# Reordering the opening transfers of a fused attention and feed-forward block, with three more fill products near its end

## The reference

```python
sa, ca, ga, sb, cb, gb = (silu(c) @ wmod) in six parts            # one row for each of 8 batches
h   = layernorm(x) * (1 + ca) + sa                                # x: (8, 512, 128), float32
q, k, v = split(h @ w_qkv.T)                                      # 16 heads of 8
p   = s(logits - max) / sum(s(...)),  logits = q @ k.T / sqrt(8)  # s: a cubic polynomial and its inverse
x   = x + gate(ga) * ((p @ v) @ w_out.T + b_out)
h   = layernorm(x) * (1 + cb) + sb
x   = x + gate(gb) * ffn(h)    # three layers of +1/-1 weights: 256 (h and -h) -> 512 -> 512 -> 128
```

## Time and profile before

| what | value |
|---|---|
| median of 3 runs | 701.52 us (701.29 to 701.98) |
| the profiled execution | 701.58 us |
| its span in the trace | 699.8 us |
| mean granted TensorE clock | 0.968 |
| VectorE busy | 641.1 us of the span |
| TensorE busy | 634.3 us |

### The profile page before, as it was taken

One profiled execution on the slowest core, in us unless ns is written; L12 is line 12 of the kernel. 1 busy time (PEld: TensorE's weight loads), 2 busy tenths in 40 slices (PEclk: granted clock), 3 DMA queues, 4 the chain that ended last, 5 costly groups with the idle time before them and its releaser, 6 DMA issues.

```text
span 699.8 us, 9639 instructions
## 1 busy us (share of the span) xinstructions
PE 634.3 (91%) x3059; PEld 253.8 (36%) x3059; DVE 641.1 (92%) x757; ACT 602.3 (86%) x622; POOL 599.0 (86%) x394
## 2 busy tenths in 40 slices
PE   6478989898889999899989999999989999997998
PEld 5123333233323343233523343233423343334366
DVE  6588999999999999999999999999999999998853
ACT  2367889998999989999999989999999989998832
POOL 8469888899989999899989999898989989797810
PEclk9575999999999999999999999999999999999999
DMA  6614112141115122332114112422214122101001
GB/s 175 193 48 166 47 53 62 61 167 46 42 40 175 49 55 78 121 107 58 51 42 168 52 54 75 151 77 58 69 43 159 43 57 72 53 10 28 16 13 31
DMA packets 37783, 53.62 MB, mean 77 GB/s; under 512 B 11308, under 2 KB 20804, under 8 KB 37732
## 3 DMA queue, kind: packets, MB, share of 16 engines
q1 hardware_dynamic: 36748, 51.81, 24.5%
q10 hardware_dynamic: 984, 1.19, 0.6%
HBM read 29.17 MB, written 18.36 MB: 68 GB/s over the span
## 4 chain that ended last, share of the span: by engine, by line
PE 55%; DVE 22%; issue 11%; ACT 8%; SPq 2%; DMA 2%; DVEq 0%; ACTq 0%
PE MB L523 13%; PE OP L601 12%; DVE mx L983 11%; PE Z L569 9%; DVE cub L974 9%; PE SA L584 8%; ACT sq L731 4%; PE MB L536 3%; PE MB L513 2%; ACT prob L745 2%; PE MB L494 1%; PE MB L611 1%; DMA parts_q<-SQ 1%; SPq L423 1%; ACT hid L786 1%
## 5 line engine op out<-in xcount | busy, mean ns | idle before, releaser
L1218 POOL TENSOR_TENSOR cub<-cub 128x2048 f32<-128x2048 f32 x127 | 456.9, 3604 | 40.1 <-DVE cub L974 39.8
L974 DVE SCALAR_TENSOR_TENSOR cub<-sq,Z 128x1024 f32<-128x1024 f32 x256 | 309.9, 1212 | 12.4 <-ACT sq L731 12.4
L731 ACT ACTIVATE sq<-Z,shift 128x1024 f32<-128x1024 f32 x256 | 282.3, 1117 | 43.7 <-PE Z L569 42.1
L983 DVE TENSOR_REDUCE mx<-SA 128x2 f32<-128x1024 f32 x248 | 302.1, 1218 | 12.6 <-PE SA L584 9.1
L745 ACT ACTIVATE prob<-cub 128x2048 f32<-128x2048 f32 x128 | 244.4, 1910 | 1.5 <-DVE cub L941 1.1
L584 PE MATMUL SA<-KH,QL 64*128 64x512 f32 x496 | 123.2, 493 | 28.8 <-DVE mx L983 25.0
L601 PE MATMUL OP<-prob,Vq 128*16 128x512 f32 x1024 | 135.1, 601 | 0.0
L569 PE MATMUL Z<-QH,KH 64*128 64x512 f32 x512 | 129.7, 503 | 5.7 <-DVE cub L974 5.5
L569 PEld LDWEIGHTS Z<-QH,KH 64*128 64x128 f32 x512 | 48.6, 186 | 183.1 <-DVE cub L974 126.8
L523 PE MATMUL MB<-hid,W 128*128 128x512 f32 x192 | 108.0, 645 | 0.0
L584 PEld LDWEIGHTS SA<-KH,QL 64*128 64x128 f32 x496 | 47.7, 188 | 109.2 <-DVE mx L983 83.6
(11 more groups left out here) (213 smaller groups left out, 526.0 us busy)
## 6 DMA issues: line engine op xcount, KB each, us to landing
QL<-parts_q SPq DMA_DIRECT2D x62, 128.0 KB, 2.6
KH<-parts_k SPq DMA_DIRECT2D x62, 128.0 KB, 2.7
QH<-parts_q SPq DMA_DIRECT2D x62, 128.0 KB, 2.7
parts_q<-SQ SPq DMA_DIRECT2D x28, 256.0 KB, 2.6
parts_k<-SK SPq DMA_DIRECT2D x28, 256.0 KB, 2.7
nd<-OT SPq DMA_DIRECT2D x124, 32.0 KB
QH<-mp SPq DMA_DIRECT2D x126, 4.0 KB
out<-y SPq DMA_DIRECT2D x7, 256.0 KB, 2.9
```

The costliest lines, as they stand in the source:

```text
L731: nc.scalar.activation(sq[:, h, :], Z[:, h, :], ACT.Square, bias=shift[:, 0:1]).then_inc(s_sq, 1)
L974: nc.vector.scalar_tensor_tensor(cub[:, m % RING, h, :], sq[:, h, :], CUB_ADD, Z[:, h, :], ALU.add, ALU.mult).then_inc(s_cv, 1)
L983: nc.vector.tensor_reduce(to, unit_bank(m, u)[:, :, :], AX_X, ALU.max).then_inc(s_mx, 1)
L1218: nc.gpsimd.tensor_tensor(ff, ff, ff, ALU.mult).then_inc(s_fp, 1)
```

## The change

The diff has these parts.

1. In SyncE's step -13, the writing of q's other quads to device memory now stands between the QL and the QH transfers of quad 0; it was after the QH transfers, the load of x and the constant rows.
2. The load of the last four batches of x moves from there to the end of SyncE's set-up, behind the weights of the layers.
3. The constant rows of QH move to step -5 (b = FIRST, n = 11), behind step -6's reads of quad 1.
4. ScalarE's squares of x run in steps -3 to 0 instead of -2 to 1, and in step -3 its two transfers of maxima stand ahead of them.
5. On VectorE, for quad 0 only, stages 1 and 2 of the combined maxima come directly behind stage 0, ahead of the reduction of unit 8; for later quads the order is the same as before. The statistics of batch 1's x move from step -15 to step -14.
6. In batch 7, steps 10 to 12 end with a fill product of 128 x 512 into SA, which waits until all maxima have been reduced.

```diff
--- before.py
+++ after.py
@@ -56,7 +56,7 @@
 AV_BEHIND = 5
 LOADS = 4
 ON_VECTOR = 3
-SQUARES_AT = (-2, -1, 0, 1)
+SQUARES_AT = (-3, -2, -1, 0)
 X_LOADS = (slice(0, 1), slice(1, 4), slice(4, B))
 M_DMAS = 4
 LEAD = 3
@@ -104,6 +104,8 @@
 FILL = {(FIRST, n): ("v", 1) for n in range(13, 16)}
 FILL |= {(0, n): ("k", 2) for n in range(2, 11)} | {(0, n): ("v", 2) for n in range(12, 16)}
 FILL |= {(1, n): ("k", 3) for n in range(2, 8)} | {(1, n): ("x1", 1) for n in range(9, 11)} | {(1, 12): ("v", 3)}
+
+FILL_LOGITS = {(B - 1, n) for n in (10, 11, 12)}
 
 
 MAIN_AT = {"xbg": 6, "wog": 5, "den_sq": 6, "den_inv": 6, "att": 7, "st2": 9, "mv2": 10, "rs2": 11, "x1n": 11,
@@ -604,6 +606,9 @@
                 mm.then_inc(s_pv, 1)
 
             def fill():
+                if (b, n) in FILL_LOGITS:
+                    pe.wait_ge(s_mx, 2 * GROUPS)
+                    nc.tensor.matmul(SA[:, 0, :], ident[:, :], W1f[:, n % KC, :], start=True, stop=True)
                 if (b, n) in FILL:
                     name, count = FILL[b, n]
                     pe.wait_ge(s_taken[name], count)
@@ -827,6 +832,9 @@
                 for i in range((B - ON_VECTOR) * TB):
                     mm = nc.scalar.activation(scratch(i), tile_of_x(i), ACT.Copy, accum_out=sum1[:, i:i + 1])
                 mm.then_inc(s_sum1, 1)
+            if s == 4 - AHEAD:
+                act.wait_ge(s_mp, 1)
+                rows_of_maxima(nc.scalar, 0, range(2, P // 32))
             if s in SQUARES_AT:
                 if s == SQUARES_AT[0]:
                     act.wait_ge(s_mean1, 1)
@@ -836,9 +844,6 @@
                                               accum_out=sq1[:, i:i + 1])
                 if s == SQUARES_AT[-1]:
                     mm.then_inc(s_sq1, 1)
-            if s == 4 - AHEAD:
-                act.wait_ge(s_mp, 1)
-                rows_of_maxima(nc.scalar, 0, range(2, P // 32))
 
         def act_tail(act):
             for g in range(2):
@@ -1040,13 +1045,18 @@
             m = s + AHEAD
             cubic(s, 0)
             of_maxima(m, 0)
+            if m == QUAD:
+                of_maxima(m, 1)
+                of_maxima(m, 2)
             maxima(m, 0)
-            of_maxima(m, 1)
+            if m > QUAD:
+                of_maxima(m, 1)
             split(b, n)
             if b == B - 1:
                 norm_late()
             cubic(s, 1)
-            of_maxima(m, 2)
+            if m > QUAD:
+                of_maxima(m, 2)
             maxima(m, 1)
             if b < B - 1:
                 norm_sums()
@@ -1068,9 +1078,8 @@
                 take_late(dve, B, "l1_3")
             if b == B and n == 2:
                 take_late(dve, B, "l1_2")
-            if b == FIRST and n == 1:
+            if b == FIRST and n == 2:
                 stats_of_x(dve, 1)
-            if b == FIRST and n == 2:
                 means_of_x(dve, 1)
                 stats_of_x(dve, 2)
                 means_of_x(dve, 2)
@@ -1340,6 +1349,7 @@
             sp.dma_start(k0u, k0.rearrange("(a p) n -> p a n", p=P)).then_inc(ld_k, 16)
             sp.dma_start(k1u, k1.rearrange("(a p) n -> p a n", p=P)).then_inc(ld_k, 16)
             sp.dma_start(k2u, k2.rearrange("(a p) n -> p a n", p=P)).then_inc(ld_k, 16)
+            load_x(sp, 2)
         def sp_step(sp, s):
             b, n = s // H, s % H
 
@@ -1358,14 +1368,8 @@
                 if beta == 0:
                     sp.wait_ge(s_zero, 2)
                     first_quad(sp, QL, "q", s_qk[0])
+                    write_parts(sp, "q", 0, OTHER_QUADS)
                     first_quad(sp, QH, "q", s_qh[0])
-                    load_x(sp, 2)
-                    sp.wait_ge(s_con, 2)
-                    sp.wait_ge(s_zero, 4)
-                    for e in range(2):
-                        r = ROWS * e + R_CON
-                        sp.dma_start(QH[r:r + 3:2, :, :].bitcast(F32), const_q).then_inc(s_rows, 16)
-                    write_parts(sp, "q", 0, OTHER_QUADS)
                 else:
                     write_parts(sp, "q", beta)
                     write_parts(sp, "k", beta)
@@ -1401,6 +1405,12 @@
                         sp.wait_ge(s_parts["k"], (beta + 1) * 4 * 16)
                     read_parts(sp, KH, parts_k, g, s_qk)
                     read_parts(sp, QH, parts_q, g, s_qh)
+            if b == FIRST and n == 11:
+                sp.wait_ge(s_con, 2)
+                sp.wait_ge(s_zero, 4)
+                for e in range(2):
+                    r = ROWS * e + R_CON
+                    sp.dma_start(QH[r:r + 3:2, :, :].bitcast(F32), const_q).then_inc(s_rows, 16)
             if b == FIRST and n == 13:
                 sp.wait_ge(s_gate, 7)
                 sp.dma_start(gate_rows, g_row).then_inc(s_gw, 16)
```

## The result

| | before | after |
|---|---|---|
| median of the runs, us | 701.38 (6 runs, 700.73 to 701.98) | 695.95 (6 runs, 693.99 to 698.39) |
| ratio, 95% interval | | 0.9926, 0.9908 to 0.9944 |
| profiled execution, us (span) | 701.58 (699.8) | 694.62 (692.7) |
| mean granted clock of that execution | 0.968 | 0.980 |

The changed kernel is faster by 5.4 us, 0.7%; 694.9 was forecast. Its runs spread over 4.4 us, those of before over 1.25. The second figure is small by luck: the 60 runs of before that were made beside the experiments lie between 698.7 and 703.4. The profiled run of after is one of its fastest, at one of its highest clocks, so the two traces differ by 7.1 us of span where the medians differ by 5.4.

A forecast was written before the change was run, and what follows sets the result against it. VectorE, busy 641.1 of 699.8 us, was taken as the bound, with losses mainly at the two ends. Terms -5.15 - 0.3 - 0.6 - 0.5 + 0 = -6.6 us on 701.58 gave 694.9 us, range 691.0 to 699.0.

The forecast's parts named there:

- Transfers: SyncE's front: quad 1's KH there at 28.0, unit 8's reduction at 28.8 instead of 33.95; -5.15 us (-6.2 to -2.9).
- Rival 2: Transfers crowded between 11 and 22 us: first unit 2 us late, unit 8 at 31.0; 697.8 us, chance 0.19.
- Rival 4: SyncE's queue blocked by x at QL's issue, quad 1 no earlier than 33; slower, 703.0 us, chance 0.04.
- Constants: SyncE, behind quad 1's reads: moving them costs nothing, with some 1.5 us of cover before the first score product at 33.4.
- VectorE's order: Quad 0: all three small stages lie in the idle time before unit 8; -0.3 us (0 to -0.4).
- squares: ScalarE: the group in step 1 goes, for which the cubic at 58.66 had waited; -0.6 us (0 to -0.7).
- Just covered: ScalarE, step -3: ten squares end at about 33.8, before the first score square needs Z at 33.9.
- Clock: TensorE, batch 0: the earlier start moves the half-clock stretch; half of one 0.95 us wait taken, -0.5 us (-2.8 to +1.5).
- Fills: Batch 7, steps 10 to 12: two hidden, the third costs 1.1 us, clock may stay up; 0 us taken.
- dip gone: Batch 7: the fills keep the clock up from 652 to 654, saving a dip of some 1.6 us; -0.5 net.
- the signs listed: Changed trace, mostly the front: expected times for x, first unit, parts_q, unit 8 and score square; later pattern 6 to 7 us earlier.
- the signs of a wrong forecast: Unit 8 after 31, first score square over 1 us behind squares, half clock past 68, or batch 7 dip with 2 us fill.

The follow-up runs named there:

- after's second series: The changed kernel itself run again, unedited, on the chip of the last experiments: 697.77 us (9 runs), ratio 0.9959 to before.
- the better version: Changed kernel with squares of x in steps -4 to -1, fills in steps 0 and 1, half fills moved or added: 692.0 us (4 runs), ratio 0.9879.

## Why the prediction held, and where it did not

*Transfers (-5.15 forecast).* The mechanism is the forecast one: the stall of 6.7 us goes, and the transfers carry all of the gain that can be told (695.94 with them alone, 700.25 with all but them). Unit 8 came 4.4 us earlier (33.95 to 29.57). Two sizes inside the term were wrong, and they partly cancelled. The delay of the first unit was taken as 0.5 us with a bound of 2; it was 1.95 in the first pair, and over all traces the first product comes at 19.2 with x in the set-up (nine traces, 18.49 to 19.79) and at 17.7 without (five traces, 17.06 to 18.23): 1.5. Part of it is a reading: the time from the end of KH's issue (15.37) to its use (17.06) is 1.7 us in the rows, and the prediction took 1 us or so; with 1.7 the same sum gives a delay of about 1.1. And parts_q, forecast to land at 23.2, never held up its readers, which were issued at 21.36; so quad 1's data were there before VectorE was through units 0 to 7, and of the 1.3 us of idle time that was to remain nothing did. From then on the first unit alone sets the front: unit 8 follows its product by 10.6 us in every trace with x in the set-up and VectorE's new order (by 10.1 with the old order). The rule of the Trainium skill weighed there ("DMA: Bandwidth & Descriptors", Issuing engines are not separate DMA queues) agrees with the traces: KH on ScalarE's queue took 3.8 us in place of 2.3 while SyncE's x moved. KH took 3.2 to 4.3 us in the eight traces in which it was issued within 4.5 us of x, 2.7 in one with 5.2 us between them, and 2.2 to 2.6 in the five in which x came later. The upper bound, which the rule pointed to, would have been the better choice.

*Rival 2, crowded transfers,* had the first unit right (2 us late) and unit 8 wrong (31.0). That its 697.8 is the median of after's second series is chance: the front of that series's trace is not the one it describes (unit 8 at 30.36). *Rival 4,* the blocked queue, did not happen: QL's issue began at 11.76 and took 2.55 us, as before, with x's megabyte ahead of it in its own queue and the DMA engines full. An issue that comes later did get longer: QH's four took 4.12 us in place of 2.65. As they took 4.13 with x behind them as well, it goes with the writes of parts_q and parts_k that now stand in front of them; by what means is not shown.

*Constants (0).* Right: issued at 25.23, and the first score product, at 34.09 (forecast 33.4), did not wait for them.

*VectorE's order (-0.3) and squares (-0.6).* These are the steps that failed, by 0.9 us in all. The order was to move the small stages into idle time ahead of unit 8, and there was none: unit 8 starts 0.47 us later against the first unit than with the old order (10.57 after 10.10), which is what the stages take, and the units behind it are no earlier. What the order does bring is a transposition 1.0 us earlier against the first unit (10.43 after 11.44).

The squares were to save the 0.66 us at the cubic of step 1. That wait was read off one trace and came from TensorE's half clock: it is absent in the trace of the fills of batch 7 alone, which has the opening of before, and in both traces with the new transfers and the old squares. There was nothing to save.

"Just covered" was said of ten squares ahead of the first score square; they were not covered. The maxima left ScalarE from 29.68 on and not from 28.1, since the first unit was later than taken, and their issue and the gap behind it took 2.4 us, so the squares ran from 32.11 to 36.0 instead of ending at 33.8. The first score square starts at 35.97, 1.4 us after its product was through (34.09 + 0.50); in before it started 0.5 us after (38.60 + 0.49, 39.60). This is over the 1 us that the prediction named as a sign of being wrong. The cubic came just as VectorE was free (35.88 + 1.23 = 37.11), so this trace shows no wait, but no cover is left either, as the 1.12 us with the small stages behind unit 8 show. Both terms together are 0 in place of -0.9.

*Clock (-0.5, bounds -2.8 to +1.5).* From quad 1 to quad 2 the traces differ by 1.7 us in favour of after. There the last half clock of the opening ended at 56.7 us, in before at 67.8. That the clock makes the whole 1.7 is argued and not shown: no run holds it fixed. In the other trace of the same code it ended at 64.0, and the span was 4.0 us longer (696.7 after 692.7): by the transpositions 0.8 in quad 0 (the first unit), 1.7 between quads 1 and 2, and 1.6 in the tail, where the clock fell from 647.7 to 651.1. So the value lay within its bounds, and it differs from run to run: after's own 15 runs lie between 694.0 and 699.9.

*Fills (0).* The sum was right, its parts were not. The fall was priced at 1.6 us and costs 0.9 (43.45 after 42.58); the third fill was priced at 1.1 at full clock and costs 0.2 (42.80 after 42.58); fills in a fall were to cost 2.1 and cost 0.9 (44.4 after 43.45). That the pair gained 0.65 us (42.80 after 43.44), near the -0.5 of "dip gone", is two errors that cancel. Alone the fills changed nothing in 12 runs.

*Sum.* In the trace: front -4.65, clock -1.7, tail -0.6, squares and order 0, together -7.0. The median, at lower clocks, gives 5.4. The forecast of -6.6 had a front too large by 0.5 to 0.8 us, 0.9 us of squares and order that were not there, and a clock term that the profiled pair exceeded. The median of after falls 1.0 us above it in the first series and 2.9 in the second; at equal clock the gain is 4.0 and 3.0 us. So the mechanism was right, and that the first number came within 1.1 us of the forecast is in part a lucky draw of the clock. Of the signs listed, parts_q by 24, unit 8 at 28 to 29.5 (29.57), the transposition ahead of it, no squares near 52 and the constant shift of 6 to 7 us came (in after's second trace the shift is 3.9). x landed at 16.9 and not by 16, the first product came at 19.0 and not by 18, the first score square at 36.0 and not by 35. The first two go with the DMA engines, full from 7 to 22 us, and with x, which was issued at 8.97 and not at 8.2; the third with the late first unit and ScalarE's order. Of the signs of a wrong forecast one came in this trace, the first score square waiting over 1 us for ScalarE's own squares, and another in after's second trace, where the clock fell in batch 7 with a fill of 1.91 us in it.

## What to carry to other kernels

Before a write that a later read depends on, count what its queue and the engines have ahead of it: the order of five transfers was worth the whole gain here, and a bulk load costs whatever stands behind it, on any queue, so it belongs where least is waited for. When a front comes forward by several microseconds, work out the cover of everything in it again from the new times, term by term: what was "just covered" is the next bound, and the better version came from moving it away. A wait that stands in one trace may belong to the clock of that execution: look for it in a second trace of the same code before it is counted as a gain. Where the clock is on the edge, spreading the filling work between the real products is worth a try; here it went with the best version, in four runs and beside the moved squares.

## What the runs showed of the hardware

- TensorE's granted clock goes to 0.5 and back at other moments in each execution. The same code had it there from 15.7 to 32.8, 43.0 to 46.5 and 49.9 to 56.7 us in one trace, from 16.2 to 33.3 and 43.5 to 64.0 in another. With VectorE as the bound, a microsecond at half clock costs only 0.18 us by the fit over all runs, but it makes most of their spread (in the 60 runs of before the two go together with a correlation of 0.88).
- The price depends on the place: 3.4 us of half clock cost 1.5 us in batch 1 at 184 us, and 0.9 in batch 7 without fills (43.45 after 42.58).
- With a DMA share of 0.94 to 1.10 from 7 to 22 us the engines moved 287 to 332 GB/s. In that stretch transfers took longer to land on either queue (KH on ScalarE's 3.8 us in place of 2.3).
- The issue of a transfer is not of one length. QL's four took 2.55 us with the engines full and x ahead in the queue, as in before; QH's four, of the same size, took 4.12 behind parts_q, and 4.13 with x not yet issued, in place of 2.65; ScalarE's four of parts_k took 4.16 in place of 2.56. Whether the queue or the engines hold the issue is not shown.
